# Hybrid conv/attention/expert block: first columns normalised apart, steps re-ordered on TensorE and ScalarE, a state mask moved to VectorE, sixteen idle products in the drain

## The chip, the cores and the metric

One Trainium2 chip; the kernel runs on one core of it. The metric is the device time of one execution in microseconds, the median of several runs. Engines are named as in the profile: PE (TensorE), ACT (ScalarE), DVE (VectorE), POOL (GpSimd), SP (SyncE, which here only issues DMAs).

## What is computed

The input x has 4 images of 32x32 positions and 128 channels, taken as B = 4 sequences of S = 1024 tokens. Three blocks follow each other, each with a residual:

```python
x = x + mlstm(group_norm(x))              # up-projection to 2 x 256, conv of 4 taps, q/k/v by blocks of 4, 8 heads
t = x.reshape(B, S, 128)
t = t + causal_attend(layer_norm(t))      # tanh scores; softmax over the earlier rows of the batch axis
t = t + experts(layer_norm(t))            # 8 experts, top 2, 128 -> 512 -> 128 with gelu
```

The first block, cut to what matters:

```python
up = xs @ W_up.T;  x_m, z = up[..., :256], up[..., 256:]
x_act = silu(conv_b + sum(xp[:, k:k+S, :] * conv_w[:, 0, k] for k in range(4)))
q, k = blocks(x_act, Wq), blocks(x_act, Wk);  v = blocks(x_m, Wv)
ig, fg = gate_in @ W_i.T + b_i, gate_in @ W_f.T + b_f
lc = cumsum(log_sigmoid(fg));  logD = where(mask, lc_i - lc_j + ig_j, -inf)
Cmat = (q @ k.T) * exp(logD - m);  h = (Cmat / norm) @ v
out = (head_norm(h) + skip * x_act) * silu(z) @ W_down.T
```

## The kernel before, in words

**Steps.** The 1024 tokens of a sequence are cut into T = 8 blocks of 128 tokens. A step t works on block t of all four sequences in the mLSTM: the scores within the block, `head(t,p)`, for eight pairs of heads and sequences-in-four; the product with the values, `values(t,p)` (L945, L955); and what earlier blocks left, a running state KV (`from_state`, `state(t,b)` L965, `new_state` L1391). Stages of other blocks run in the same step: the q/k/v products and gates of block t+1 (`qkv`, `gate_rows`, `queries`, `gate_cols`), the up-projection of block t+3 (`up`, L867), the head norm and down-projection of block t−1 (`turn_heads`, `down`), the attention of block t−2 and t−3 (`attn_turn`, `attn_fc`, `attn_score`, `rows_turn`, `logits`), and the routing of block t−4 (`counts`, L1008 to L1014), whose rows ScalarE writes scaled into `xrow` (`send_rows`, L623) and GpSimd scatters with indirect DMAs to a list by expert in DRAM (`scatter`, L1983).

**Order.** Nothing is planned at run time. Each engine has a hand-written program, a function `step(t)` of its own for PE, ACT, DVE and POOL, which says in which order the parts are issued; semaphores tie the engines together. Small products of PE share two PSUM banks `pG` in turn. The class `Ring` (L78) lists all uses of those banks in the order in which they come (`STEP`, by name and lag, and `DRAIN`); a use can be claimed when the engine that reads the use two places before has freed the bank. So the order in `STEP` has to be that of PE's program, and what ends a wait of PE at a claim is the reader of the bank two uses back.

**Opening.** The input is loaded transposed into `xT` (128 channels by 4 x 1024 tokens), its statistics are made, and DVE normalises it in place, one operation for each sequence (L1291, semaphore `xn_ready`). PE then waits for `xn_ready`, for `tables_made` (of DVE) and for `pool_tables_made` (of POOL, which fills `w` with a memset, L1932, and makes masks), and computes `up(0)` and `up(1)`. DVE folds norms into weights (`kg`, L1294), does the conv of block 0 (L1323), and waits for the gates.

**Gates of a block.** ACT copies q, k, v out of PSUM (`qkv(t,b)`), then gate inputs, then `q_copy` and `q_diagonal` (L566, q spread by head into `w`), then the exponentials `gate_exps` (L572). DVE works on the gates (`gate`, L1336 to L1351, scans and minima on 32 rows), on `gate_cols`, and on `qprime` (L1363, which takes `uq`). PE turns the gate inputs (`gate_rows`, L890). The eight products of score and decay per step are DVE's `weigh(t,p)` (L1382).

**State mask.** In each step but the last, POOL multiplies KV by a head mask into `KVm` (`masked_state`, L1966 to L1971), for PE's `from_state` of the next step. Its order in POOL's step: `values_scaled` (vs, L1955), head norm rstd, `scatter` in two halves with `masked_state` between them, `skipped` (sx, L1963), rstd again.

**Drain and experts.** After step 7 PE does what is left of attention and routing, `attn_score(5)` to `counts(7)` (L1148 to L1169), two idle products of resident weights among it (`warm(pA[0], 2)`, L1168; a `warm` is a product of 128 x 512 whose result nobody reads, L919). `list_firsts` begins the list of expert tiles. The DVE side is `places` (L1545, adds the counts to the offsets), the POOL side `scatter`. Then come the expert tiles (L1186, L1199) in rounds, and at last the sum of both experts' rows.

Of the kernel before, what the change touches and what calls it, by code (L numbers as in the profile page):

```python
# [19 lines left out]
ALU = mybir.AluOpType  # L20
# [7 lines left out]
P = 128  # L28
B = 4
C = 128  # L30
S = 1024
# [46 lines left out]
class Ring:  # L78
# [30 lines left out]
def block_kernel(nc, a, out):  # L109
    ctx = ExitStack()  # L110
    with ctx:
# [352 lines left out]
        def _(act):  # L464
# [136 lines left out]
            def square(t, f):  # L601
                act.wait_ge(sem("half_copied"), 4 * t + 2 * f + 2)
                nc.scalar.activation(dsq[:, f], osb[:, f, :, :, 0:DH], ACT.Square).then_inc(sem("dsq_done"), 1)
# [71 lines left out]
            def step(t):  # L675
# [30 lines left out]
                if nxt:  # L706
                    qkv(t + 1, 1)
                    qkv(t + 1, 2)
                if four:
                    send_rows(t - 4)  # L710
                if now:
                    out_copy(t, 0)
                    square(t, 0)
                if nxt:
# [3 lines left out]
                if nxt:  # L718
                    gate_inputs(t + 1)
                    q_copy(t + 1)  # L720
                    q_diagonal(t + 1, 0)
                if now:
# [84 lines left out]
        def _(pe):  # L807
# [229 lines left out]

            pe.wait_ge(sem("xn_ready"), B)
            pe.wait_ge(sem("tables_made"), 1)
            pe.wait_ge(sem("pool_tables_made"), 1)  # L1040
            up(0, 0, ("xm0", "xm1"))
            up(1, 0, ("xm0", "xm1"))
            for b in range(B):
# [5 lines left out]
            head(0, 0)  # L1049
            gate_turn(0)  # L1050
            up(2, 0, ("xm0", "xm1"))

            def step(t):
# [19 lines left out]
                if nxt:  # L1073
                    state(t, 2)
                    state(t, 3)
                    qkv(t + 1, 0)
                if now:
                    values(t, 2)
                if four:
                    counts(t - 4)  # L1080
# [7 lines left out]
                if now:  # L1088
                    values(t, 3)
                if one:  # L1090
                    turn_heads(t - 1, 1)
                if now:
                    head(t, 5)
                if nxt:
                    qkv(t + 1, 3)
                    gate_rows(t + 1)
# [49 lines left out]
            for t in range(T):  # L1146
                step(t)
            attn_score(5)  # L1148
            attn_turn(6)
            counts(4)  # L1150
            turn_heads(7, 0)
            turn_heads(7, 1)
            attn_fc(6)
            down(7)
            attn_score(6)
            rows_turn(5)
            logits(5)
            attn_turn(7)
            counts(5)
            attn_fc(7)  # L1160
            attn_score(7)
            rows_turn(6)
            logits(6)
            counts(6)
            rows_turn(7)
            logits(7)
            list_firsts()
            warm(pA[0], 2)  # L1168
            counts(7)  # L1169
# [68 lines left out]
        def _(dve):  # L1238
# [50 lines left out]
            dve.wait_ge(sem("gr_done"), 1)  # L1289
            for b in range(B):  # L1290
                v.tensor_scalar(xT[:, b, :], xT[:, b, :], gm[:, b:b + 1], gr[:, b:b + 1], ALU.subtract, ALU.mult  # L1291
                                ).then_inc(sem("xn_ready"), 1)
            bank, read = arrived(dve, None, "geffx")
# [91 lines left out]
            def new_state(t, b):  # L1385
                if b == 0:
                    dve.wait_ge(sem("state_ready"), t + 1)
                    taken(dve, t, "uq1")
                bank, read = arrived(dve, t, f"st{b}")
                for f in range(HALVES):  # L1390
                    v.scalar_tensor_tensor(KV[:, f * B + b, :], KV[:, f * B + b, :], decay[:, f, b:b + 1],  # L1391
                                           bank[:, f * HPH * DE:(f + 1) * HPH * DE], ALU.mult, ALU.add
                                           ).then_inc(*((read, 1) if f else (sem("state_part"), 1)))

            def norm_a(t, f):
# [190 lines left out]
            for f in range(HALVES):  # L1586
                conv(0, f)
                halo(1, f)
            gate(0)
            gate_cols(0)  # L1590
# [3 lines left out]
            def step(t):  # L1594
# [63 lines left out]
                if one:  # L1658
                    residual(t - 1)
                if nxt:  # L1660
                    gate_cols(t + 1)
                if t + 2 < T:
# [204 lines left out]
        def _(pool):  # L1867
# [97 lines left out]

            def masked_state(t):  # L1966
                taken(pool, t, "st3")
                pool.wait_ge(sem("state_used"), 2 * t + 2)
                g.tensor_tensor(KVm[:, :, :], KV[:, :, :],  # L1969
                                bc(headmask[:, :, :].rearrange("p h d -> p (h d)"), 1, HALVES * B),  # L1970
                                ALU.mult).then_inc(sem("state_ready"), 1)  # L1971

            def rsqrt(ap, n, ready, count, done):
# [22 lines left out]
            def step(t):  # L1996
# [10 lines left out]
                if three:  # L2007
                    row_scale(t - 3)
                if nxt:
                    masked_state(t)  # L2010
                if four:
# [66 lines left out]
```

## Time and profile before

| What | us |
|---|---|
| median of 3 runs | 636.13 (633.67 to 636.51) |
| the profiled execution, device time | 638.62 |
| its span in the trace | 636.8 |
| mean granted clock of PE | 0.904 of full |
| PE busy | 528.5 (83%) |
| DVE busy | 461.0 (72%) |
| ACT busy | 366.7 (58%) |
| POOL busy | 281.0 (44%) |
| chain that ended last: PE, DVE, ACT, issue, DMA, POOL | 47%, 22%, 10%, 8%, 7%, 2% |

All times of rows and of stretches come from the profiled execution, counted from the start of its span. It is 2.5 us longer than the median. The shares are means over stages that differ: the opening (to about 60 us), eight steps (to about 420 us), the drain (to about 460 us), the expert tiles and the final sum.

### The profile page before, as it was taken

What the parts mean: (1) busy time and instruction counts of PE and PEld (TensorE: products, weight loads), DVE (VectorE), ACT (ScalarE), POOL (GpSimd) and SP (SyncE); (2) the same over time, 40 slices, a digit from 0 to 9 for tenths busy, and PEclk for the clock granted to TensorE, in tenths of its full rate; (3) what the DMA queues carried; (4) which work ended last, traced back from release to release, by engine and by line L of the source; (5) the groups of instructions that cost most, each with busy time, mean ns of one, the idle gap of its engine ahead of it and who ended that gap; (6) DMA issues with size and microseconds to landing.
All of it is one profiled execution on the core that took longest, in us unless ns stands there. A gap on an engine that the chain in (4) does not pass through costs nothing.

```text
span 636.8 us, 12714 instructions
## 1 busy us (share of the span) xinstructions
PE 528.5 (83%) x3370; PEld 411.3 (65%) x3371; DVE 461.0 (72%) x1467; ACT 366.7 (58%) x924; POOL 281.0 (44%) x289
## 2 busy tenths in 40 slices
PE   5568999999998998989889988564598999999940
PEld 3444766667656666667567656443398899999940
DVE  8625667776777869979968785798776677776726
ACT  5166768676575686685765862643354555555520
POOL 7711025222251252753653726564755444444530
PEclk9569999999999999999999997765589999999985
DMA  6000000000000000000000501400232222222219
GB/s 167 33 2 0 1 0 1 2 1 0 1 2 0 1 2 10 26 1 14 22 1 18 150 0 33 138 30 18 77 97 66 63 60 65 64 62 68 67 63 338
DMA packets 34574, 28.08 MB, mean 44 GB/s; under 512 B 6823, under 2 KB 30265, under 8 KB 34528
## 3 DMA queue, kind: packets, MB, share of 16 engines
q1 hardware_dynamic: 24288, 16.45, 9.3%
q0 software_dynamic: 4352, 8.47, 3.7%
q10 hardware_dynamic: 5888, 2.62, 1.4%
q8 instruction: 21, 0.34, 0.2%
q14 instruction: 25, 0.20, 0.1%
HBM read 16.36 MB, written 11.67 MB: 44 GB/s over the span
## 4 chain that ended last, share of the span: by engine, by line
PE 47%; DVE 22%; ACT 10%; issue 8%; DMA 7%; POOL 2%; SPq 1%; DVEq 1%; POOLq 0%; ACTq 0%
PE pO L1199 6%; PE pO L955 4%; PE pS L936 4%; PE pS L1186 3%; DVE x_tok L1487 3%; PE pA L1186 3%; ACT w L566 3%; PE pG L867 2%; PE pG L897 2%; PE pO L945 2%; DVE cacc L1323 2%; DVE PT L1382 2%; DMA ktok<-expert_out 2%; PE pG L877 2%; DMA expert_out<-yT,vext 1%
## 5 line engine op out<-in xcount | busy, mean ns | idle before, releaser
L955 PEld LDWEIGHTS pO<-vext,PT 128*128 128x128 f32 x512 | 64.3, 193 | 25.7 <-DVE PT L1382 18.8
L955 PE MATMUL pO<-vext,PT 128*128 128x33 f32 x512 | 65.1, 272 | 9.1 <-DVE PT L1382 9.1
L936 PE MATMUL pS<-w,xact 128*128 128x512 f32 x128 | 66.5, 601 | 0.0
L790 ACT ACTIVATE sz<-pA,b1f 128x128 f32<-128x128 f32 x144 | 41.2, 368 | 40.7 <-PE pA L1186 40.7
L1975 POOL TENSOR_TENSOR rs<-rs,mhalf 128x4 f32<-128x4 f32 x16 | 16.4, 1024 | 104.4 <-DVE rs L1500 55.2
L1975 POOL TENSOR_TENSOR var<-var,mhalf 128x16 f32<-128x16 f32 x16 | 49.2, 3075 | 29.4 <-DVE var L1414 29.4
L1983 POOL DMA_INDIRECT expert_rows<-xrow,slot x48 | 49.2, 1025 | 26.2 <-issue 11.8
L790 ACT ACTIVATE sx<-pS,b1f 128x128 f32<-128x128 f32 x144 | 41.2, 367 | 33.3 <-PE pS L1186 31.8
L591 ACT ACTIVATE D<-pA 128x512 f32<-128x512 f32 x64 | 38.1, 595 | 36.9 <-PE pA L931 36.4
L2041 POOL DMA_INDIRECT expert_out<-yT,vext x36 | 35.3, 982 | 45.7 <-DVE yT L1812 44.5
L1382 DVE TENSOR_TENSOR PT<-pS,D 128x512 f32<-128x512 f32 x64 | 44.0, 687 | 10.2 <-ACT D L591 7.1
L2041 POOL DMA_INDIRECT expert_out<-yT,vs x36 | 35.7, 991 | 28.7 <-DVE yT L1812 19.5
L1792 DVE TENSOR_SCALAR osb<-pG,lngbT 128x128 f32<-128x128 f32 x72 | 29.5, 410 | 24.2 <-PE pG L1176 15.9
L1323 DVE SCALAR_TENSOR_TENSOR cacc<-xm,convw,cacc 128x512 f32<-128x512 f32 x48 | 39.3, 819 | 6.4 <-ACT cacc L496 5.1
L566 ACT ACTIVATE w<-qT 32x512 f32<-32x512 f32 x64 | 39.9, 623 | 1.2
L1969 POOL TENSOR_TENSOR KVm<-KV,headmask 128x1056 f32<-128x1056 f32 x7 | 16.9, 2415 | 53.3 <-PE pO L945 53.3
L1199 PE MATMUL pO<-w,sz 128*128 x288 | 39.0, 279 | 0.4 <-DVE firstrow L1731 0.4
L1199 PE MATMUL pO<-w,sx 128*128 x288 | 38.2, 276 | 0.0
L867 PE MATMUL pG<-xT,wupT 128*128 128x512 f32 x64 | 36.9, 696 | 0.5 <-issue 0.5
L1808 DVE TENSOR_TENSOR qpT<-pO,b2b 128x128 f32<-128x128 f32 x72 | 20.8, 289 | 22.6 <-PE pO L1199 20.4
L1199 PEld LDWEIGHTS pO<-w,sz 128*128 128x128 f32 x288 | 35.9, 196 | 0.6 <-issue 0.6
L1199 PEld LDWEIGHTS pO<-w,sx 128*128 128x128 f32 x288 | 35.0, 192 | 0.4 <-issue 0.4
(348 smaller groups left out, 1399.2 us busy)
## 6 DMA issues: line engine op xcount, KB each, us to landing
vs<-expert_rows SPq DMA_DIRECT2D x36, 65.0 KB, 1.8
vext<-expert_rows SPq DMA_DIRECT2D x36, 65.0 KB, 1.9
x_tok<-in_x SPq DMA_DIRECT2D x8, 256.0 KB, 5.4
w<-in_L_ffn_W SPq DMA_DIRECT2D x8, 256.0 KB, 4.7
w<-in_L_ffn_W SPq DMA_DIRECT2D x1, 2048.0 KB, 9.4
xT<-expert_out SPq DMA_DIRECT2D x4, 512.0 KB, 4.9
out<-x_tok ACTq DMA_DIRECT2D x8, 256.0 KB, 7.0
expert_rows<-xrow,slot POOLq DMA_INDIRECT x48, 2.4
```

The lines of the kernel that those rows point to most:

```text
L566: nc.scalar.activation(qbd2[t % 2][rows, f, :, h, :], qT[rows, f], ACT.Copy).then_inc(sem("diagonal_made" if h == HPH - 1 else "copied_par ...
L790: nc.scalar.activation(hidT[u % 2][:, k, :], bank[:, ROWS * (k % 2):ROWS * (k % 2 + 1)], ACT.Gelu, bias=b1f[:, u % WBUFS, k:k + 1]).then_i ...
L867: mm(bank[:, :], wupT[:, lo + f, :], xT[:, :, P * t:P * t + P], start=True, stop=True).then_inc(written, 1)
L936: mm(pS[n % 2][:, :], xact2[t % 2][:, f, b, :], qbd2[t % 2][:, f, b].rearrange("p h i -> p (h i)"), start=True, stop=True).then_inc(sem("s ...
L955: last = mm(pO[b // 2][:, o:o + DE], PT[:, n % 2, h, :], vext2[t % 2][:, b, HPH * f + h, :], start=False, stop=True, skip_group_check=True)
L1186: last = mm(bank[:, ROWS * (k % 2):ROWS * (k % 2 + 1)], w1f[u % WBUFS][:, P * k:P * k + P], xeT[:, u % WBUFS, :], start=True, stop=True)
L1199: last = mm(o, hidT[u % 2][:, k, P * j:P * j + P], w2[:, bass.ds(e, 1), k, :].rearrange("p e c -> p (e c)"), start=(k == 0), stop=(k == FK ...
L1323: v.scalar_tensor_tensor(cacc[:, f], xm2[t % 2][:, f, :, k:k + P], convw[:, f, k:k + 1], cacc[:, f], ALU.mult, ALU.add).then_inc(sem("tap_ ...
L1382: v.tensor_tensor(PT[:, h % 2].rearrange("p b i -> p (b i)"), pS[h % 2][:, :], D[:, h % 2].rearrange("p b i -> p (b i)"), ALU.mult).then_i ...
L1975: g.tensor_tensor(ap, ap, mhalf[:, 0:n], ALU.pow).then_inc(sem(done), 1)
L1983: g.indirect_dma_start(xs, bass.IndirectOffsetOnAxis(slots[side(s)][:, k, b:b + 1].bitcast(U32), 0), xrows[side(s)][:, b, k, :], None).the ...
L2041: g.indirect_dma_start(y2, bass.IndirectOffsetOnAxis(xin[u // 4][:, u % 4, j, C + 1:C + 2].bitcast(U32), 0), yout[:, u % OUTS, j, :], None ...
```

## The change

It has five parts.

- *First columns.* DVE normalises the first 256 columns of each sequence (two blocks) and goes on; the other 768 columns follow after the conv of block 0. `xn_ready` counts to 8 instead of 4. PE does `up(0)` and `up(1)` behind `xn_ready` 4 and ahead of the waits for the tables; `up(2)` waits for `xn_ready` 8.
- *PE's step.* `values(t,2)` is issued ahead of `qkv(t+1,0)`, and `qkv(t+1,3)` ahead of `turn_heads(t-1,1)` and `head(t,5)`; in the ring k3 and v3 come ahead of y1.
- *ACT's step.* `out_copy(t,0)` comes first, then `qkv(t+1,3)`, `exps(t,5)`, `gate_inputs`, `square(t,0)`, `q_copy`, and then `send_rows(t-4)`, which stood ahead of them all.
- *State mask.* `masked_state(t)` goes from POOL to DVE, behind `residual(t-1)` and ahead of `gate_cols(t+1)`.
- *Drain.* Sixteen idle products in place of two, in eight places.

```diff
-            ("k1", 1), ("v1", 1), ("k2", 1), ("v2", 1), ("y1", -1),
-            ("k3", 1), ("v3", 1), ("gateT", 1), ("q0", 1), ("q1", 1),
+            ("k1", 1), ("v1", 1), ("k2", 1), ("v2", 1), ("k3", 1), ("v3", 1), ("y1", -1),
+            ("gateT", 1), ("q0", 1), ("q1", 1),
...
@@ ACT, step @@
                     qkv(t + 1, 2)
+                if now:
+                    out_copy(t, 0)
+                if nxt:
+                    qkv(t + 1, 3)
+                if now:
+                    exps(t, 5)
+                if nxt:
+                    gate_inputs(t + 1)
+                if now:
+                    square(t, 0)
+                if nxt:
+                    q_copy(t + 1)
                 if four:
                     send_rows(t - 4)
-                if now:
-                    out_copy(t, 0)
-                    square(t, 0)
-                if nxt:
-                    qkv(t + 1, 3)
-                if now:
-                    exps(t, 5)
-                if nxt:
-                    gate_inputs(t + 1)
-                    q_copy(t + 1)
+                if nxt:
                     q_diagonal(t + 1, 0)
@@ PE, opening @@
             pe.wait_ge(sem("xn_ready"), B)
+            up(0, 0, ("xm0", "xm1"))
+            up(1, 0, ("xm0", "xm1"))
             pe.wait_ge(sem("tables_made"), 1)
             pe.wait_ge(sem("pool_tables_made"), 1)
-            up(0, 0, ("xm0", "xm1"))
-            up(1, 0, ("xm0", "xm1"))
...
             gate_turn(0)
+            pe.wait_ge(sem("xn_ready"), 2 * B)
             up(2, 0, ("xm0", "xm1"))
@@ PE, step @@
                     state(t, 3)
+                if now:
+                    values(t, 2)
+                if nxt:
                     qkv(t + 1, 0)
-                if now:
-                    values(t, 2)
...
                     values(t, 3)
+                if nxt:
+                    qkv(t + 1, 3)
                 if one:
                     turn_heads(t - 1, 1)
                 if now:
                     head(t, 5)
                 if nxt:
-                    qkv(t + 1, 3)
                     gate_rows(t + 1)
@@ PE, drain @@
             attn_score(5)
+            warm(pA[0], 2)
             attn_turn(6)
             counts(4)
             turn_heads(7, 0)
             turn_heads(7, 1)
+            warm(pA[0], 1)
             attn_fc(6)
             down(7)
             attn_score(6)
+            warm(pA[0], 2)
             rows_turn(5)
             logits(5)
+            warm(pA[0], 1)
             attn_turn(7)
+            warm(pA[0], 1)
             counts(5)
             attn_fc(7)
             attn_score(7)
             rows_turn(6)
             logits(6)
+            warm(pA[0], 5)
             counts(6)
+            warm(pA[0], 1)
             rows_turn(7)
             logits(7)
             list_firsts()
-            warm(pA[0], 2)
+            warm(pA[0], 3)
             counts(7)
@@ DVE @@
-            for b in range(B):
-                v.tensor_scalar(xT[:, b, :], xT[:, b, :], gm[:, b:b + 1], gr[:, b:b + 1], ALU.subtract, ALU.mult
-                                ).then_inc(sem("xn_ready"), 1)
+            def normalized(columns):
+                for b in range(B):
+                    v.tensor_scalar(xT[:, b, columns], xT[:, b, columns], gm[:, b:b + 1], gr[:, b:b + 1],
+                                    ALU.subtract, ALU.mult).then_inc(sem("xn_ready"), 1)
+            normalized(slice(0, 2 * P))
...
+            def masked_state(t):
+                taken(dve, t, "st3")
+                dve.wait_ge(sem("state_used"), 2 * t + 2)
+                v.tensor_tensor(KVm[:, :, :], KV[:, :, :],
+                                bc(headmask[:, :, :].rearrange("p h d -> p (h d)"), 1, HALVES * B),
+                                ALU.mult).then_inc(sem("state_ready"), 1)
...
                 halo(1, f)
+            normalized(slice(2 * P, S))
             gate(0)
...
                     residual(t - 1)
                 if nxt:
+                    masked_state(t)
                     gate_cols(t + 1)
@@ POOL: the same masked_state taken out, and its call between scatter(t - 4, (0,)) and scatter(t - 4, (1,)) @@
```

## Rows read from the trace of the kernel before

**Rows 1.** The page, part 2: granted clock in 40 slices of 15.9 us
```profile
PEclk9569999999999999999999997765589999999985
```

**Rows 2.** Timeline of DVE and POOL, opening (start us, us, engine, line) and line L1291
```profile
22.96 4.13 DVE L1291 TENSOR_SCALAR xT<-xT,gm,gr 128x1024 f32<-128x1024 f32 x1 [1.17 <-POOL gr L1930]
L1291 DVE TENSOR_SCALAR xT<-xT,gm,gr x4: 796/802/4131, 23.0 to 28.5; 128x1024 f32<-128x1024 f32 x4
22.89 3.51 POOL L1932 MEMSET w<- 128x4096 f32 x1
29.18 0.16 DVE L1294 COPY kg<-pG 128x16 f32<-128x16 f32 x1
38.30 2.32 DVE L1323 SCALAR_TENSOR_TENSOR cacc<-xm,convw,cacc 128x512 f32<-128x512 f32 x3
53.17 0.21 DVE L1336 TENSOR_SCALAR fmin<-gpre 32x128 f32<-32x128 f32 x1 [12.28 <-issue]
```

**Rows 3.** Timeline of PE, opening
```profile
30.67 6.67 PE L867 MATMUL pG<-xT,wupT 128*128 128x512 f32 x8 [0.47 <-issue]
```

**Rows 4.** Timeline of PE in the steps: products after a wait
```profile
72.38 0.51 PE L877 MATMUL pG<-kg,xact 128*128 128x144 f32 x2 [0.64 <-ACT xact L511]
109.11 0.48 PE L877 MATMUL pG<-kg,xact 128*128 128x144 f32 x2 [0.35 <-DVE KV L1391]
119.82 0.38 PE L890 MATMUL pG<-ident,gates 128*32 128x128 f32 x2 [0.64 <-ACT gatesm L535]
240.30 0.48 PE L877 MATMUL pG<-kg,xact 128*128 128x144 f32 x2 [1.53 <-DVE KV L1391]
244.99 0.51 PE L877 MATMUL pG<-kg,xact 128*128 128x144 f32 x2 [0.39 <-DVE offs L1548]
```

**Rows 5.** Timeline of ACT in the steps
```profile
116.26 0.67 ACT L598 ACTIVATE osb<-pO 128x264 f32<-128x264 f32 x2 [0.35 <-PE pO L955]
248.13 1.70 ACT L623 ACTIVATE xrow<-xt,rs 128x256 f32<-128x256 f32 x4
257.48 2.57 ACT L566 ACTIVATE w<-qT 32x512 f32<-32x512 f32 x4
```

**Rows 6.** Timeline of DVE and POOL in the steps, and one group of DVE
```profile
256.96 3.28 DVE L1351 TENSOR_TENSOR fmin<-lc,g 32x128 f32<-32x128 f32 x1
131.72 0.28 DVE L1363 TENSOR_TENSOR uq<-uq 32x128 f32<-32x128 f32 x1 [1.28 <-ACT uq L572]
257.69 2.41 POOL L1969 TENSOR_TENSOR KVm<-KV,headmask 128x1056 f32<-128x1056 f32 x1
L1382 DVE TENSOR_TENSOR PT<-pS,D 128x512 f32<-128x512 f32 x64 | 44.0, 687 | 10.2 <-ACT D L591 7.1 <-PE pS L936 2.5
```

**Rows 7.** Timeline of POOL and PE around the start of step 5
```profile
265.30 2.24 POOL L1963 TENSOR_SCALAR sx<-xact,vecs 128x512 f32<-128x512 f32 x2
276.06 1.96 POOL L1955 TENSOR_TENSOR vs<-vext,gtok 128x1056 f32<-128x1056 f32 x1
279.84 1.06 PE L965 MATMUL pG<-vs,ktok 128*128 128x132 f32 x8
```

**Rows 8.** Drain and first expert tiles: timelines, then one stretch by windows
```profile
423.33 1.09 PE L994 MATMUL pG<-ident,xt 128*128 128x128 f32 x4 [2.60 <-ACT xt L615]
445.87 0.19 PE L1008 MATMUL pG<-selb,before 128*128 128x32 bf16 x1 [5.62 <-DVE selb L1540]
451.96 3.62 PE L919 MATMUL pA<-xT,wupT 128*128 128x512 f32 x4
455.91 0.19 DVE L1545 TENSOR_TENSOR pos<-pG,offs 128x32 f32<-128x32 f32 x1 [0.62 <-PE pG L1014]
460.93 1.92 PE L1186 MATMUL pA<-osb,D 128*128 128x128 f32 x8
468.52 1.06 PE L1186 MATMUL pS<-osb,xact 128*128 128x128 f32 x8
422.80:460.60 37.80, 19.28 (x92) 13.03 (x92) 30.65 (x155) 15.14 (x37) 24.58 (x25) 0.50 0.15 43
```

More of the change, by code:

```diff
@@ L708, in step @@
                     qkv(t + 1, 2)
-                if four:
-                    send_rows(t - 4)
                 if now:
                     out_copy(t, 0)
-                    square(t, 0)
                 if nxt:
@@ L719, in step @@
                     gate_inputs(t + 1)
+                if now:
+                    square(t, 0)
+                if nxt:
                     q_copy(t + 1)
+                if four:
+                    send_rows(t - 4)
+                if nxt:
                     q_diagonal(t + 1, 0)
@@ L1075, in step @@
                     state(t, 3)
-                    qkv(t + 1, 0)
                 if now:
                     values(t, 2)
+                if nxt:
+                    qkv(t + 1, 0)
                 if four:
@@ L1964, in skipped @@
                                     ).then_inc(sem("sx_ready" if f else "waits_apart"), 1)
[L1966 to L1971, printed above, removed]
             def rsqrt(ap, n, ready, count, done):
@@ L2008, in step @@
                     row_scale(t - 3)
-                if nxt:
-                    masked_state(t)
                 if four:
```

## The prediction

> **What bounds the kernel now.** I read the page first, then PE's waits, then the timelines stage by stage. The clock line [rows 1] shows stages: slices 4 to 24 (48 to 382 us) at full, 25 to 27 falling, 28 and 29 (430 to 461) at half, which is 1.2 of 2.4 GHz, and from 31 on (478) full again for the expert tiles. In the steps (60 to 420 us) PE is the engine that is almost always busy, so a wait of PE there counts if nothing else ends the step. The timeline of PE shows the waits that the diff aims at: 0.47 us before the first products of the kernel [rows 3], and in the steps 0.64, 0.35, 0.64, 1.53 and 0.39 us [rows 4]. ACT and DVE are close behind [rows 5, 6]. The drain, 422.8 to 460.6, is a chain of short links between DVE, ACT, POOL and PE: PE works 19.28 of 37.80 us at clock 0.50 [rows 8].
>
> **The change, part by part.**
>
> *The first columns.* Today four DVE operations on 1024 columns each stand before PE's first product. The first took 4.13 us, the others 0.80 [rows 2]: it started at 22.96, POOL's memset ran from 22.89 to 26.40, and the excess of 3.33 is close to that memset's length. So I don't scale the first operation by its columns: the hold to 26.4, then about 0.2 us (a quarter of 0.80) for each of four, all done near 27.25 instead of 29.25: −2.0. By columns alone it would be some −5 (4.13 to about 1.0, the others 0.80 to 0.20). The Trainium skill (SBUF — State Buffer, "Who interferes with whom") says that DVE's two-port operations and GpSimd take the port pair that they share exclusively, and the later one is blocked for the whole instruction; by that rule too it is −2.0 and not −5. PE's 0.47 [rows 3] goes with the tables' wait, which now stands behind up(1). Sum −2.45. The copy of kg that followed [rows 2] comes sooner too. The second part, four operations of about 0.6 us (2.4 in all), sits before gate(0), where DVE idles 12.28 us until 53.17 [rows 2]; the third conv tap and what precedes it keep their place. Cost 0, and 2.4 if that cover were gone. up(2) waits for it, long after. Bounds: 0 (PE's products of block 0 then wait for something else of the opening), and the −5.
>
> *PE's order in a step.* values(t,2) goes ahead of qkv(t+1,0). At t=0 it fills ACT's xact wait: −0.64; at t=1 to 3 it fills the 0.35 wait on KV, −0.35 each [rows 4]. At t=4 to 6 the wait is 1.53 [rows 4], but there the count bank follows, which DVE reads late (0.39 behind), in a stretch where DVE is never free: values(t,2) early only moves the wait; 0. qkv(t+1,3) goes ahead of turn_heads(t−1,1) and head(t,5), and the bank ring follows (k3, v3 before y1). That closes the wait of 0.64 for gatesm [rows 4], seven times. What is late next: y1 now takes the bank behind k3 and v3, which must have been copied by ACT, and ACT does out_copy (0.67) first [rows 5]; I put the new wait at about 0.35, half of that copy, so −0.3 a step remains at t=0 to 3. Bounds: −0.64 and nothing.
>
> *ACT's order.* Moving out_copy(t,0) and qkv(t+1,3) ahead, send_rows(t−4) behind q_copy. The work is the same. For t=4 to 6 send_rows, 1.70 us [rows 5], now runs in front of q_diagonal(t+1,0) (2.57 [rows 5]) instead of some 8 us earlier. ACT sets the end there: q_diagonal to gate_exps to uq, which DVE awaits (1.28 [rows 6]). The gain of the gates' inputs is paid back there; I take t=4 to 6 as 0. On POOL, the eight DMA issues of scatter(t−4) come behind send_rows, so they start later; the ends I place at 272.3 for sx against its user on ACT at 272.9 (sx ran from 265.30 [rows 7]), and at 278.2 for vs, which ended at 278.02 against PE's use at 279.84 [rows 7]. SP's queue is passed by nothing. So margins of 0.6 and 1.8: 0.
>
> Steps in sum: −0.64 − 3×0.35 − 4×0.3 = −2.9. Bounds: −7 if every closed wait is gained whole (0.64 + 6×0.35 + 7×0.64), +2 if y1's wait is the whole 0.67 in four steps and send_rows costs in one.
>
> *The mask on DVE.* It leaves POOL (2.41 us, seven times) and comes to DVE before gate_cols(t+1) [rows 6]. On DVE I price it by columns from the product PT<-pS,D of L1382, 687 ns for 512: 1056 columns come to 1.42, bound from below by 1.28, which is the wait it lies in [rows 6]. weigh(t,6) is over by then, and the following weigh is behind uq's wait, so 0 at t=0 to 3. The other side: while POOL's mask ran from 257.69, DVE's operation of L1351 that is else short took 3.28 [rows 6]. That delay falls away, yet uq, due from ACT, ended later anyway. 0; bounds −1.1 a step at t=4 to 6 (what weigh(6) was late by it, the 3.28 less the 2.2 of waiting behind) and +0.14 a step (1.42 − 1.28).
>
> *The idle products of the drain.* Sixteen instead of two. A product of 512 columns at half clock is 1.71 us (group of 3.62 for two, with its load [rows 8]). The gaps they fill: 2.60 before the turn of xt, 5.62 before selb's counts [rows 8]. Two places don't fit: five before counts(6) are 8.55 against 5.62, late by 2.93 at half clock and inside it (4.3) at full; the third before counts(7) adds 1.71 on DVE's path, since DVE already waits 0.62 for PE there [rows 8]; the rest together at most 1.6. So at half clock throughout +6.2; part of it is covered because PE idles again before the first tiles, and part comes back where the clock rises inside the dense stretch (turns and attn_fc(7) in half the time, about 0.9). Followed through the drain's waits, the 1.6 vanishes in waits of PE for ACT and POOL, and of the 2.93 + 1.71 about half (2.2), since ACT's and POOL's part of the chain is not later than before: 6.2 − 1.6 − 2.2 − 0.9 = +1.5, which I take. Bounds −4.1 (clock at full everywhere, no product late) and +6.2. First tiles: the group of eight at half clock takes 1.92, at full 1.06 [rows 8]; PE stands still over 3 us before them whatever is filled in, so I leave them at half.
>
> Sum: −2.45 − 2.9 + 0 + 1.5 = −3.85, on 638.62, the profiled execution's time (span 636.8 and 1.8 around it): 634.8. The median of the three runs is 636.13, 2.5 below that execution, so **632.3**.
>
> **The rivals.** (A) *The clock stays up.* The clock fell at the start of the drain, when PE's gaps began [rows 1], and in its stretch PE is busy half the time [rows 8]; with 14 products more, 14×1.71 = 24 us of work at half clock or 12 at full, it would be much busier. The Trainium skill (TensorE: Matmul & The Clock Gate, "HAM oscillation") says that the clock follows how busy PE has been and drops in gaps. By that rule idle products pay. Worked out from the rows: the five fit, of the 19.28 us of products 9.6 would go, a third of it (3.2) on the chain, and the first tiles save 0.86 in their group; together −4.1 instead of +1.5: 626.7. For: the clock only fell where PE's gaps began; against: many of the gaps stay open, and the clock was 0.50 through a stretch with PE half busy. 0.13. (B) *Slower: send_rows starves POOL.* Place: t=4 to 6, scatter's issues behind send_rows. If vs is late by more than its 1.8, PE's state(t+1,0) waits, and sx the same on ACT. Price: rows start 8 us later where I count 0.2 of effect; of the 8, 2.4 is the mask's time that POOL gets back, 1.8 the margin and 1.3 idle time of POOL ahead of its rows, which leaves 2.5 a step in three steps, +7.3: 639.6. It decides from a vs 1.8 late on. For: the margins of 0.6 and 1.8 are thin. Against: POOL loses its 2.41 mask in the same steps. 0.08. (C) *The waits only move.* y1 waits for ACT as long as gatesm did, and DVE ends the step. Then −2.45 + 1.5 = −0.95: 635.2. For: ACT and DVE waits of the same size stand behind [rows 5, 6]. 0.25. (D) *POOL's hold was on the path.* The 3.28 of L1351 did delay weigh(6): 1.1 in three steps on top: 629.0. Against: the ACT-bound wait of uq behind it. 0.12. My forecast keeps 0.42, its own range 629.5 to 634.5.
>
> **How the numbers follow.** A measurement here can tell about 0.5% (3.2 us) from no change: faster is under 632.95, slower over 639.3. The forecast lies mostly just under the line: of its 0.42 about 0.27 faster, 0.15 same. A and D are faster (0.25), C is same but for 0.03, B splits, 0.05 slower; small mishaps of the drain near its +6.2 add 0.02. Faster 0.55, same 0.38, slower 0.07. Range: from 627.5, which leaves out A's lower part (0.1), to 636.8, which leaves out B and the top of C (0.1).
>
> **What would show it.** PE's first product at 28.2 or so instead of 30.67; if at 30, the columns part is wrong. In the steps the wait on gatesm gone and one of about 0.35 before the turn of y1; if that wait is 0.6, (C). DVE's L1351 back to short at every step and KVm on DVE at 1.3 to 1.4 us; a later PE wait on PT would mean it isn't covered. vs ending before PE's state; a wait there is (B). In the drain, PE's 5.62 gone, DVE's wait before pos (L1545) grown from 0.62 to about 2, and the granted clock still near 0.5; a clock near 1 is (A).

## The result: 1.0% slower

The changed kernel took 642.62 us (median of 4 runs, 641.95 to 643.63) against 636.32 before (4 runs, 633.67 to 637.05): ratio 1.0102, 95% interval 1.0071 to 1.0132. Forecast were 632.3 and a range to 636.8. Its profiled execution took 641.95, with a span of 639.5. Single runs over 1.5% above the fastest of the same kernel are left out of every ratio.

The two traces side by side, starts in us (before / after): PE's first product 30.67 / 28.04; the turn of the gates of block 5 at 252.21 / 247.49, of block 6 at 298.92 / 295.07, of block 7 at 346.09 / 345.27; counts(6) 445.87 / 446.74, counts(7) 455.44 / 456.53; the third tile of round 1 482.14 / 483.55; the span's end 636.8 / 639.5. So the change was 4.7 us ahead at t=4 (2.6 of it from the opening), lost 3.9 of it by block 7, and then was later. The device time outside the span also grew, from 1.8 to 2.5 us. The spans differ by 2.7 and the medians by 6.3, because the traced execution of before is 2.3 us over its median, that of after 0.7 under its own, and 0.6 of the difference lies outside the span.

The page of after, its first row and that of the granted clock:

```profile
span 639.5 us, 12775 instructions
PEclk9579999999989999999879998866798999999985
```

The clock in the drain did rise: counted from 1, slices 25 to 29 are 8, 8, 6, 6, 7 where they were 7, 7, 6, 5, 5 [rows 1]. But the row has three digits under 9 in the steps (slices 12, 20 and 21, at 176 and 304 to 336 us) where before had none, and an 8 in slice 31, among the tiles (480 to 496).

The opening, timelines of DVE and PE of after (start us, us, engine, line, operation):

```profile
22.48 4.69 DVE L1306 TENSOR_SCALAR xT<-xT,gm,gr 128x256 f32<-128x256 f32 x4 [1.17 <-POOL gr L1956]
28.04 5.84 PE L870 MATMUL pG<-xT,wupT 128*128 128x512 f32 x8
```

All four column operations were over at 27.17 (27.25 was forecast, [rows 2]); the hold by POOL's memset (22.41 to 25.92 here) is still in them. PE's wait of [rows 3] is gone.

The steps: waits of PE in after, and ACT and DVE at the end of step 6.

```profile
72.89 0.51 PE L880 MATMUL pG<-kg,xact 128*128 128x144 f32 x2 [0.90 <-ACT gates L527]
234.84 1.08 PE L958 MATMUL pO<-vext,PT 128*128 128x33 f32 x8 [0.91 <-DVE PT L1399]
325.89 1.92 PE L958 MATMUL pO<-vext,PT 128*128 128x33 f32 x8 [2.01 <-DVE PT L1399]
350.57 1.70 ACT L623 ACTIVATE xrow<-xt,rs 128x256 f32<-128x256 f32 x4
355.39 0.69 DVE L1399 TENSOR_TENSOR PT<-pS,D 128x512 f32<-128x512 f32 x1 [4.25 <-ACT D L591]
356.14 1.08 PE L958 MATMUL pO<-vext,PT 128*128 128x33 f32 x8 [0.40 <-DVE PT L1399]
L1368 DVE TENSOR_TENSOR fmin<-lc,g x8: 268/270/271, 52.0 to 349.3; 32x128 f32<-32x128 f32 x8
L1415 DVE TENSOR_TENSOR KVm<-KV,headmask x7: 1249/1250/1253, 87.9 to 356.7; 128x1056 f32<-128x1056 f32 x7
```

At t=0 the wait of 0.64 [rows 4] became one of 0.90. At t=4 to 6 the waits of 1.53 on KV [rows 4] became waits of 0.91, 0.91 and 2.01 on DVE's weighted scores: values(t,2), now first, needs a product of DVE that is not there. The one of 2.01 us is longer than the wait that it replaced. The product behind it took 1.92 instead of 1.08: in windows of 1 us the granted clock is 0.50 from 326 to 332 and was 1.00 before. The same is so at 237 to 240, behind the wait of 0.91 at 234.84. At the end of step 6 send_rows is the row ahead of q_diagonal, ACT's exponentials of pair 6 come behind both, and DVE stood 4.25 us for them.

The drain, one stretch by windows (as in [rows 8]), and single rows:

```profile
422.80:460.60 37.80, 27.37 (x112) 14.99 (x110) 28.89 (x149) 14.64 (x34) 23.86 (x25) 0.73 0.16 45
439.40 7.51 PE L922 MATMUL pA<-xT,wupT 128*128 128x512 f32 x10
452.30 4.40 PE L922 MATMUL pA<-xT,wupT 128*128 128x512 f32 x6
447.20 0.19 DVE L1569 TENSOR_TENSOR pos<-pG,offs 128x32 f32<-128x32 f32 x1 [1.59 <-PE pG L1017]
456.99 0.19 DVE L1569 TENSOR_TENSOR pos<-pG,offs 128x32 f32<-128x32 f32 x1 [1.39 <-PE pG L1017]
```

The clock of the stretch rose from 0.50 to 0.73, and DVE, which had waited only once for PE's counts in this stretch (0.62, [rows 8]), now waited three times: 1.14, 1.59 and 1.39. The five products before counts(6) took 7.51 us, between half and full clock.

### The profile page after: what moved, and what is told of

Read it like the earlier page. It is cut to its first block, busy times and chain, and to the rows that moved or that the text cites. A ratio compares the mean times of both kernels' runs of the same rounds, so it can differ in the third digit from the quotient of the medians.

```text
span 639.5 us, 12775 instructions
## 1 busy us (share of the span) xinstructions
PE 543.8 (85%) x3398; PEld 413.9 (65%) x3399; DVE 454.3 (71%) x1478; ACT 366.0 (57%) x924; POOL 265.0 (41%) x282
## 4 chain that ended last, share of the span: by engine, by line
PE 47%; DVE 18%; ACT 10%; issue 9%; DMA 8%; POOL 4%; SPq 2%; DVEq 1%; POOLq 0%; ACTq 0%
PE pO L1212 6%; PE pO L958 5%; PE pS L939 4%; PE pS L1199 3%; PE pA L1199 3%; PE pA L922 3%; ACT w L566 3%; PE pG L900 2%; PE pO L948 2%; DMA expert_out<-yT,vext 2%; DVE x_tok L1511 2%; DMA ktok<-expert_out 2%; PE pG L870 2%; POOL expert_rows L2002 2%; DVE cacc L1340 1%
## 5 line engine op out<-in xcount | busy, mean ns | idle before, releaser
L939 PE MATMUL pS<-w,xact 128*128 128x512 f32 x128 | 69.3, 624 | 0.0
L870 PE MATMUL pG<-xT,wupT 128*128 128x512 f32 x64 | 34.6, 655 | 0.0
L939 PEld LDWEIGHTS pS<-w,xact 128*128 128x128 f32 x128 | 25.7, 201 | 10.5 <-issue 1.4
```

What stands on the lines that cost most here:

```text
L870: mm(bank[:, :], wupT[:, lo + f, :], xT[:, :, P * t:P * t + P], start=True, stop=True).then_inc(written, 1)
L939: mm(pS[n % 2][:, :], xact2[t % 2][:, f, b, :], qbd2[t % 2][:, f, b].rearrange("p h i -> p (h i)"), start=True, stop=True).then_inc(sem("s ...
```

## The experiments

Each line of times is a median; the ratio is to the kernel before on the same chip, with its 95% interval. The ratio isn't the quotient of the two medians, and the two can differ by 0.4% (values_back: 1.0027 by the medians, 1.0063 by the ratio). So differences of medians below are good to some 2 us, and where it matters the difference by the ratios stands beside them. "Outside the span" is the device time less the span, the median of the runs, in us. The first eight ran on one chip (before: 636.96 for the first four, 636.56 for the next), the rest on three others.

| kernel | us | ratio | outside the span |
|---|---|---|---|
| before_again | 635.92 | 1.0004 (0.9969 to 1.0039) | 1.79 |
| no_idle | 635.91 | 0.9998 (0.9971 to 1.0025) | 1.78 |
| idle_alone | 638.96 | 1.0043 (1.0012 to 1.0074) | 2.74 |
| values_back | 638.66 | 1.0063 (1.0030 to 1.0096) | 2.55 |
| tiny_idle | 641.24 | 1.0057 (1.0020 to 1.0094) | 2.60 |
| mix1 | 634.38 | 0.9959 (0.9926 to 0.9992) | 1.80 |
| rows_early | 637.59 | 1.0018 (0.9986 to 1.0051) | 2.56 |
| cols_alone | 633.70 | 0.9965 (0.9933 to 0.9997) | 1.79 |
| tiny_double | 655.77 (before 654.82) | 1.0045 (1.0005 to 1.0085) | 1.86 |
| tiny_before | 655.87 (654.82) | 1.0034 (0.9992 to 1.0076) | 2.60 |
| cols_mask | 651.99 (654.82) | 0.9989 (0.9952 to 1.0026) | 1.80 |
| cols_order | 652.14 (654.82) | 0.9985 (0.9949 to 1.0021) | 1.81 |
| no_idle_2 | 656.06 (654.19) | 1.0035 (0.9999 to 1.0072) | 1.77 |
| tiny_idle_2 | 655.46 (654.19) | 1.0034 (1.0001 to 1.0068) | 2.60 |
| tiny_double_2 | 652.61 (654.19) | 0.9985 (0.9950 to 1.0020) | 1.87 |
| idle_shift | 655.94 (654.19) | 1.0048 (1.0019 to 1.0078) | 1.86 |
| tiny_double_3 | 656.83 (656.10) | 1.0008 (0.9974 to 1.0042) | 1.83 |
| idle_shift_2 | 657.11 (656.10) | 1.0027 (0.9992 to 1.0062) | 1.84 |

**Whole or without the idle products.** no_idle puts the drain's PE program back to two idle products; idle_alone puts the new drain into the kernel before; values_back swaps two calls:

```diff
-                if now:
-                    values(t, 2)
                 if nxt:
                     qkv(t + 1, 0)
+                if now:
+                    values(t, 2)
```

> The kernel before, unchanged, for a second trace. Its first trace was 638.62 us, 2.3 above the median of its other runs (636.3). Theory 1 (PE's granted clock falls to half after single waits of PE, at places that differ from run to run): this trace shows other or fewer stretches at half clock in the steps than the first (three, 13.7 us together). Theory 2 (the expert tiles' loads land earlier or later): the stretches are the same and the wait of PE for vs near 480 us (1.53) differs by over 1 us. Ratio to before 1.00 within 0.2%.

> The change with the drain's idle products put back to the two of before. Theory A (the idle products cost: five before counts(6) and the third before counts(7) are late at half clock, 2.0 us ahead at 408 us became 1.1 us late at 456): 3 us faster than the change, 639.6, and 4.5 faster (638) if the wait for the loads near 480 goes too. Theory B (they held the clock up and so paid for themselves; the loss is in the steps alone): same as the change, 642.6, or slower.

> The kernel before with only the sixteen idle products in the drain. Theory A: slower than before by 3 to 4.5 us, 639.3 to 640.8. Theory B: 636.3 or less.

> The change with values(t,2) behind qkv(t+1,0) again, as before. Theory C (values(t,2) ahead of the q/k/v products waits for DVE's product of that pair, up to 2.01 us at t=6, and these waits brought half clock at 237 and at 326 us, 9.8 us of it, so 4.9 us): 3 to 5 us faster than the change, 638 to 640, and no half clock near 326. Theory D (the half clock comes from any wait of that size, wherever it stands): the KV wait of 1.53 is back and the time is within 1 us of the change, 642.6.

Without the fourteen the whole gap is gone: 635.9, further down than either theory had it. In the kernel before the same fourteen cost only 2.0 us on the median (638.96 to 636.96), 2.7 by the ratio; in the change they cost 6.7 (642.62 to 635.91, 6.6 by the ratios). Theory A had the sign right, not the reason: DVE's late counts explain about 1 us in the traces (from the gates of block 7 to counts(7): 110.1 us in no_idle, 111.3 in after), and the rest came later. values_back took 4.0 off the change (2.5 by the ratios, whose intervals overlap, so this gain isn't clear of noise), and its trace has no half clock near 326; the wait on KV is back, and the clock stayed full behind it. That speaks against theory D in this one trace:

```profile
324.84 1.08 PE L958 MATMUL pO<-vext,PT 128*128 128x33 f32 x8 [1.07 <-DVE PT L1399]
330.33 0.48 PE L880 MATMUL pG<-kg,xact 128*128 128x144 f32 x2 [1.53 <-DVE KV L1408]
```

(values_back, timeline of PE.) But other traces speak for it. The unchanged kernel's second trace, before_again, has the same wait on KV with a lower clock behind it (timeline of PE, then the windows before and behind the wait; the granted clock is the third number from the end):

```profile
240.77 0.48 PE L877 MATMUL pG<-kg,xact 128*128 128x144 f32 x2 [1.53 <-DVE KV L1391]
236.00:241.00 5.00, 3.47 (x23) 2.54 (x23) 4.79 (x21) 3.59 (x6) 1.38 (x1) 1.00 0.00 0
242.00:246.00 4.00, 4.00 (x28) 2.78 (x28) 3.93 (x14) 1.28 (x4) 0.00 (x0) 0.61 0.01 2
```

cols_alone, mix1 and idle_alone have it at the same place too, while the first trace of before [rows 4] and values_back have the wait and a full clock behind it. So the same wait is followed by half clock in some executions and not in others, and theory D is open.

As for the two theories of before_again, the first holds: its stretches of half clock lie elsewhere than in the first trace (12.2 us of them in 60 to 400 us, at 147, 242 and 317 among others, against 13.7 at 190, 316 and 388), and the wait near 480 is the same (1.55 against 1.53). before_again also shows what the spread of this kernel is: over its twelve runs the time goes with the granted clock of the run, 632.55 at 0.919 and 639.39 at 0.900.

**Instructions without work.** tiny_idle keeps the fourteen added products, each 4 columns wide instead of 512 (the added calls pass columns=1):

```diff
-            def warm(bank, n):
+            def warm(bank, n, columns=P):
                 for _ in range(n):
-                    mm(bank[:, :], wupT[:, 0, :], xT[:, :, 0:P], start=True, stop=True)
+                    mm(bank[:, 0:B * columns], wupT[:, 0, :], xT[:, :, 0:columns], start=True, stop=True)
```

> The change with its fourteen added idle products narrowed from 512 to 4 columns each: as many instructions of PE, hardly any work. Theory F (the longer instruction stream of PE shifts its fetches: in the three kernels with the added products one fetch of 0.02 MB on the queue q8 fell at 476.0 to 478.5, into the rows' way to the first tiles of round 1, where without them it falls at 482.0 to 483.5; PE then waited 2.24 to 2.60 us for vs near 481 instead of 1.48 to 1.55, the clock fell behind that wait, and the time outside the span was 2.5 to 2.7 instead of 1.8): fetch near 476 to 479, the wait over 2 us, half clock near 481 to 484, and 2.5 us or so outside the span; median 638 to 639, against 635.9 without any of the fourteen. Theory G (the idle work itself costs, by delaying counts(6) and counts(7) and by moving the clock): fetch or not, 635.9 as without them, and 1.8 outside the span.

This run separates the instructions from their work. With hardly any work the fourteen cost 5.3 us by the medians (641.24 against 635.91) and 3.8 by the ratios, whose intervals overlap only from 1.0020 to 1.0025. It isn't so in every run: four of the twelve took 634.6 to 637.2, as without the fourteen (632.5 to 638.0). The traced one took 642.57. Up to the tiles the two traces agree: counts(7) at 455.3 in no_idle, 455.4 in tiny_idle. Then the chain that ended last, in no_idle and in tiny_idle:

```profile
476.92 2.27 DMA expert_out<-yT,vs
479.93 1.72 DMA vs<-expert_rows
481.77 0.32 PE pG L1182
```

```profile
477.18 3.41 DMA expert_out<-yT,vs
481.32 1.76 DMA vs<-expert_rows
483.20 0.47 PE pG L1190
```

The transfer that the load of the third tile waits for took 3.41 us instead of 2.27. The queues of tiny_idle between 477.5 and 479.5 us show what else was under way (packets, MB, share of 16 engines):

```profile
q0 software_dynamic: 56, 0.10, 15.4%
q8 instruction: 1, 0.02, 4.0%
```

In no_idle the row of q8 isn't there in that window; its fetch falls at 483. In after the fetch is at 478.5 and the same transfer took 3.41; in idle_alone 476.0 and 2.95; in values_back 477.5, where the load behind it took 2.69 instead of 1.8. In rows_early, below, it is 477.5, and that load took 2.34. PE then stood over 2 us where it had stood 1.5, and the products behind ran at half clock, in all five traces with the fourteen and in none of the five without (tiny_idle, then no_idle, timelines of PE):

```profile
483.20 0.47 PE L1190 MATMUL pG<-ident,vs 128*128 128x128 f32 x1 [2.64 <-DMA vs<-expert_rows]
483.46 1.93 PE L1200 MATMUL pA<-osb,D 128*128 128x128 f32 x8
485.18 1.60 PE L1213 MATMUL pO<-w,sx 128*128 x8
```

```profile
481.77 0.32 PE L1182 MATMUL pG<-ident,vs 128*128 128x128 f32 x1 [1.48 <-DMA vs<-expert_rows]
481.93 1.11 PE L1192 MATMUL pA<-osb,D 128*128 128x128 f32 x8
482.88 1.06 PE L1205 MATMUL pO<-w,sx 128*128 x8
```

So 1.4 us at the wait, 2.8 when the next tile begins (486.6 against 483.8), 4.6 at the tiles around 510 (514.2 against 509.6), 5.2 at the end. 1.23 of it is one more wait for a load, at 497.97; the first trace of before has one there too (1.02 at 497.10), so that wait doesn't need the fourteen.

**The steps' parts.** rows_early is the change with send_rows ahead of out_copy again; mix1 has that too, values(t,2) back, and the two idle products of before; cols_alone is the kernel before with the columns alone.

```diff
+                if four:
+                    send_rows(t - 4)
                 if now:
                     out_copy(t, 0)
...
                     q_copy(t + 1)
-                if four:
-                    send_rows(t - 4)
-                if nxt:
                     q_diagonal(t + 1, 0)
```

> The change without the added idle products, with values(t,2) behind qkv(t+1,0) and with send_rows(t-4) at its old place. Theory H (the change's first columns and the rest of its order are a gain of 5 us that values(t,2), send_rows and the idle products gave back, 1.0 to 1.2 us a step at t=4 and 6 for send_rows): 631 to 633. Theory I (the steps' gain is paid back in the last step and the drain, whatever the order): 635.9 as without the idle products alone.

> The change with send_rows(t-4) at its old place. Theory J (send_rows ahead of q_diagonal holds the chain to uq: the turn of the gates of block 7 to the attention product of step 6 took 18.7 us instead of 17.5, that of step 4 21.2 instead of 20.2): these two stretches are back at 17.5 and 20.2, the time 2 to 3 us below the change, 640. Theory K (it is covered): stretches 18.7 and 21.2, 642.6.

> The kernel before with only the first columns apart. If the 2.0 to 2.6 us that PE's first product gained are kept to the end: 634 to 634.5. If the opening gives them back: 636.5. PE's first product at 28.0 to 28.8 either way.

cols_alone keeps what the opening gains: 2.9 us, ratio clear of 1. rows_early is 5.0 under the change (5.3 by the ratios, intervals apart). Its stretch to the attention product of step 6 is 17.5 us again as in theory J (342.8 to 360.3), that of step 4 is 19.6. DVE's idle time there fell:

```profile
351.30 0.69 DVE L1398 TENSOR_TENSOR PT<-pS,D 128x512 f32<-128x512 f32 x1 [2.64 <-ACT D L591]
```

The two edits also act on each other: the wait of 2.01 us on DVE at t=6 is 0.92 in rows_early, with the clock full behind it, although values(t,2) is as early as in the change.

```profile
329.20 0.97 PE L957 MATMUL pO<-vext,PT 128*128 128x33 f32 x7 [0.92 <-DVE PT L1398]
```

But the parts don't add up. Both put back without the idle products, mix1, give 634.4, only 1.5 under no_idle and no better than the columns alone. Two things can be seen in the traces. With send_rows at its old place the first product of y1 waits for ACT, for 1.17 to 1.20 us at t=4 to 6 of mix1 and about as long in rows_early; neither before nor the change has that wait.

```profile
248.03 0.66 PE L1025 MATMUL pG<-ident,hn 128*128 128x128 f32 x4 [1.17 <-ACT gates L527]
```

And the clock of 60 to 400 us differs, by windows of cols_alone, no_idle and mix1 in turn:

```profile
60.00:400.00 340.00, 310.23 (x1855) 219.59 (x1853) 265.10 (x768) 233.70 (x528) 139.53 (x95) 0.99 0.07 20
```

```profile
60.00:400.00 340.00, 317.08 (x1836) 222.69 (x1834) 254.16 (x763) 227.27 (x519) 121.60 (x86) 0.96 0.05 14
```

```profile
60.00:400.00 340.00, 314.54 (x1839) 221.57 (x1838) 253.80 (x770) 228.78 (x523) 126.66 (x87) 0.97 0.06 17
```

PE's busy time is 4 to 7 us more, for 16 to 19 recorded products fewer, at 0.96 to 0.97 instead of 0.99 of full clock. These are single traces, and the two of the kernel before lie between (312.79 and 312.18 us busy, at 0.98). The time at half clock in these 340 us goes with it: 7.5 us in cols_alone, 13.7 and 12.2 in before, 20.5 in mix1 and in the change, 23.9 in no_idle, but only 10.3 in values_back. Over all runs the mean granted clock is 0.911 in before and in cols_alone, 0.908 in mix1 and 0.906 in no_idle. So the gains of the new order seem to be paid back in part as slow products; what sets where the clock falls is open.

**Mask and order by themselves, and a longer stream.** cols_mask and cols_order are cols_alone with the mask on DVE, and with the order on PE and ACT (values(t,2) and send_rows at their old places). tiny_double has twenty-eight narrow products, tiny_before puts the fourteen into the kernel before. On this chip PE waits far longer near 480 (4.1 to 6.6 us in one piece), so the times compare only by ratio.

> The kernel before with the first columns apart and the state mask on DVE, nothing else. If the mask is covered on DVE and POOL's hold cost nothing, as forecast: 633.7, as with the columns alone. If DVE pays for it (1.3 us a step where it is not covered): 635 to 640. If POOL's hold was on the path at t=4 to 6 (rival D): 630.4.

> The kernel before with the first columns apart and the order of the change on PE and ACT, but values(t,2) and send_rows at their old places and the mask on POOL. By the forecast for that part (−0.3 a step at t=0 to 3): 632.5. If the closed wait for gatesm only moved (rival C): 633.7. With the mask on DVE as well it was 634.4.

> The change with twenty-eight added idle products of 4 columns in place of its fourteen of 512: PE's instruction stream longer by twice as much. If what counts is where the fetch falls (Theory F): it moves by the same step again, from 478.0 (fourteen) and 483.0 (none) to about 473, ahead of the rows' way to the tiles; the wait of PE near 481 is back near 1.5 and the time below the 641.2 of fourteen, about 637. If what counts is the number of instructions, wherever their fetch falls: 646 or more, the wait 3 or more. The time outside the span is 1.8 if it hangs on a fetch's place, 3.4 if on the length.

> The kernel before with the fourteen added products of 4 columns. Theory F: fetch at 476 to 478, wait of PE near 481 at 2.2 to 2.6 us, 640 to 642 against 636.6, and 2.6 us outside the span. Theory that the effect is one of the change's other edits: 636.6.

Neither mask nor order adds to the columns: 0.9989 and 0.9985 against 0.9965, all within each other's intervals, though on two different chips. For the mask that is +0.24%, give or take 0.49%: a cost of 7 times 1.3 us (1.4% of the time) is excluded, and so is the gain of 3.3 us (0.5%) that rival D forecast; a cost of up to 0.7% is not. tiny_before is 0.34% over before with 1 inside its interval, which decides nothing. tiny_double, twenty-eight narrow products, is 0.45% over before and clear of 1, but the change without any of them did not run on this chip. One thing is plain: the time outside the span is 1.8 with none, 2.6 with fourteen and 1.86 with twenty-eight, so it doesn't grow with the number of instructions.

**The dose once more.**

> The change without the fourteen added idle products, again, as the zero of the dose series on this chip: ratio to before 1.000 within 0.3%, 1.8 us outside the span, PE's wait for vs before the third tile of round 1 about 1.5 us if the chip is like the first.

> Fourteen added products of 4 columns, again. Cause 1 and cause 2 both: 4 to 5 us above the zero (the first time 641.2 against 635.9), 2.6 us outside the span.

> Twenty-eight added products of 4 columns. Cause 1 (the fetch's place): fetch ahead of the rows' way, the wait back at 1.5 us, 1.8 us outside the span and within 1.5 us of the zero. Cause 2 (number): twice the loss, 8 to 10 us above the zero.

> The change as it is, with fourteen more products of 4 columns beside the idle ones, so as long a stream as with twenty-eight. Cause 1: 4 to 5 us faster than the change although it does more, so about 0.2% to 0.4% over before, and 1.8 us outside the span. Cause 2: 1.0% over before, or more.

On this chip none and fourteen are the same (1.0035, 1.0034) and twenty-eight are 0.5% faster. The wait that the fourteen had lengthened is there already, and the products behind it run at half clock in all four kernels (no_idle_2, then tiny_idle_2, timelines of PE):

```profile
485.58 0.47 PE L1182 MATMUL pG<-ident,vs 128*128 128x128 f32 x1 [6.41 <-DMA vs<-expert_rows]
```

```profile
485.36 0.47 PE L1190 MATMUL pG<-ident,vs 128*128 128x128 f32 x1 [5.17 <-DMA vs<-expert_rows]
```

The load itself isn't slow here: in no_idle_2 it took 1.88 us (1.72 in no_idle), but it started at 483.66 instead of 479.93, behind a chain of SP's own work. SP's writes of the lists' tails, which stand ahead of it, took 12.44 us instead of 8.34 and ended 10.7 us later (no_idle_2, then no_idle, timelines of SP's queue):

```profile
469.61 12.44 SPq L435 DMA_DIRECT2D expert_rows<-tail  x8
463.00 8.34 SPq L435 DMA_DIRECT2D expert_rows<-tail  x8
```

Why SP is slower on this chip no run shows.

The number of instructions as such (cause 2) falls on this chip: twenty-eight were expected 8 to 10 us above none and are 3.4 below, and idle_shift is at 1.0048, where 1.0% or more was expected. It says nothing on the place of the fetch, since the long wait is there without any added product. The work of the idle products is idle_shift less tiny_double_2, as long a stream in both: 3.3 us here, 4.1 by the ratios.

> Twenty-eight narrow products. If this chip is like the first (before near 636): by the place of the fetch within 1.5 us of the 635.9 without any, PE's wait near 481 at 1.5 us and 1.8 us outside the span; by the number of instructions 645 or more. If it is like the second and third (before near 654): ratio 0.998 to 1.005 and nothing decided.

> The whole change with fourteen narrow products more. On a chip like the first: by the place 637 to 639, by the number 645 or more, against 642.6 for the change. On one like the second: 1.005.

The last chip was again of the slower kind (before 656.1): 1.0008 and 1.0027, the idle work 0.3 us on the medians (1.2 by the ratios). Twenty-eight have not run on a chip like the first. That the place of the fetch, and not something else that fourteen more instructions shift, lengthened the wait there is thus supported by five traces with the fetch in the transfers' way and waits of 2.09 to 2.64 us (after, idle_alone, values_back, tiny_idle, rows_early) and five without and 1.42 to 1.55, and not shown by moving it: the five with are just the five kernels that have fourteen more products. And it can't be the whole of the 5.3 us: idle_alone has the fetch in the way and a wait of 2.24 with half clock behind it, and costs 2.0 to 2.7 us with the work of its products included.

## Why the prediction was wrong

- *First columns, −2.45:* right. 2.9 in cols_alone, interval 0.2 to 4.3; the hold by the memset was in the row as the working had it.
- *PE's order and ACT's order, −2.9 in sum:* wrong, measured +2.2 with the mask (no_idle 635.9 less cols_alone 633.7; 0.33% by the ratios, whose intervals overlap, so the loss isn't clear of nothing, but the gain of 2.9, 0.46%, is excluded). To t=4 the one trace of the change gains 2.1 us beside the opening; t=4 to 6, which the sum took as 0, lose 3.9. Two steps of it failed. "values(t,2) early only moves the wait; 0" was right about the move and wrong about the price: the wait on DVE was 2.01 at t=6 in the place of 1.53, and half clock stood behind it for over 6 us. It has that price only with send_rows late: with send_rows at its old place the wait is 0.92. And "I take t=4 to 6 as 0" for send_rows: put back to its old place in the change, it gives 5.0 us. From the gates' turn to the attention product of the step it is 18.7 us instead of 17.5 at t=6, 21.2 instead of 20.2 at t=4. What send_rows was late for was not POOL (rival B) but ACT's exponentials of pair 6, which stand behind q_diagonal, and at t=4 also ACT's copy of xm, for which PE waits 1.71 us at 258.12 in the change (1.70 in no_idle and values_back, none in rows_early, mix1 and before). The forecast price of y1, a wait of 0.35, isn't in the trace of the change, and it is 1.2 at t=4 to 6 where send_rows is early; the wait for gatesm is gone.
- *Mask on DVE, 0:* right as far as measured (+0.24%, give or take 0.49%). 1.25 us an operation, POOL's hold gone from all of DVE's short ones (3.28 to 0.27), and nothing won by it, so rival D falls.
- *Idle products, +1.5:* too small; taken out of the change they give 6.7 us back. For their work alone +1.5 is within what was measured: 1.4 us by the medians and 2.9 by the ratios between tiny_idle and the change on the first kind of chip, 3.3 (4.1) and 0.3 (1.2) on two others. Rival A half came: the clock in the drain rose to 0.73, and the time still didn't fall, because what the drain waits for is ACT and DVE. But the sum had no term for the longer stream of instructions: with next to no work the fourteen cost 5.3 us (3.8 by the ratios), in the traces 5.2 within the span, in the expert tiles, where nothing had been changed, and 0.8 outside it. By what way is open.

By those terms: −2.9 + 2.2 + 5.3 + 1.4 = +6.0, against +6.3 measured. That the sum closes proves nothing: each term is one median less the next along a chain from before to the change, so it must. In another order the parts have other prices: send_rows and values(t,2) put back give 1.5 us without the idle products, and send_rows alone 5.0 with them; the fourteen cost 2.0 in the kernel before and 6.7 in the change. Rival B had the right sign and the right instruction, send_rows behind its old place, but the wrong engine: PE's waits for vs are no longer than before, and what came late was ACT.

## What to carry to other kernels

Idle products that fill TensorE's waits are not free even where they fit. Run them once with next to no work, as tiny_idle does, and look at the stage that follows as well as at their own; here the instruction queue's fetch beside its transfers is a suspect, not a shown cause. A reordering that closes a wait of an engine is worth what the next wait is shorter, and where the moved instruction waits itself, its wait can bring a slower clock with it: read the granted clock in fine windows behind the longest waits, in more than one trace, before counting the gain. Parts of a change that meet in the same waits have no price of their own; measure them in the company in which they will run. Of this change the first columns alone are worth keeping, 0.35% (0.03 to 0.67), and mix1 gives the same, 0.41% (0.08 to 0.74).

## What was not expected of the hardware

- Fourteen products of 4 columns made the kernel 5.3 us slower on one chip (3.8 by the ratios) and made no difference on another (1.0035 and 1.0034).
- One fetch of 0.02 MB on q8 beside a scattered write of the result rows went with 3.41 us for it instead of 2.27.
- The same wait of PE, 1.53 us on KV at t=4, had half clock behind it in four traces (before_again, cols_alone, mix1, idle_alone) and full clock in two (before, values_back).
- Chips differ: the same kernel before took 636.6 on one and 654.2 to 656.1 on three, with single waits of PE of 4.1 to 6.6 us near 480 in place of 1.5. In no_idle_2 the load that ended the wait took 1.88 us and was issued late by SP.
- The time outside the span went 1.8, 2.6, 1.86 us with none, fourteen and twenty-eight added products. Why is open.
